# Attention with latent keys on one core: the second part of each exchange issued by ScalarE instead of SyncE

## The reference

```python
q = (x @ wq.T).reshape(B, S, N_HEADS, QK_HEAD)            # QK_HEAD = 128 + 64
q_lat = jnp.einsum('bshd,hdc->bshc', q_nope, wkv_b_h[:, :NOPE])
kv_cache = rmsnorm(kv_lat, kv_norm_w)
scores = (q_lat . kv_cache + q_pe . k_pe) * SCALE          # both einsums over t
attn = jax.nn.softmax(jnp.where(causal, scores, NEG_INF), axis=-1)
out_lat = jnp.einsum('bsht,btc->bshc', attn, kv_cache)
out = jnp.einsum('bshc,hdc->bshd', out_lat, wkv_b_h[:, NOPE:])
return x + out.reshape(B, S, N_HEADS * VDIM) @ wo.T + ffn(xn)
```

## Time and profile before

| | |
|---|---|
| median of 3 runs | 2135.69 us (2128.77 to 2140.19) |
| the profiled execution | 2143.6 us, its span 2141.6 us |
| TensorE's granted clock, mean | 0.915 of 2.4 GHz |
| busy share of the span | PE 84%, DVE 57%, POOL 47%, ACT 40% |
| exchange copies (L943) | 1536, all issued by SyncE: 256 of 64 KB, 768 of 128 KB, 512 of 96 KB |
| DMA queue of SyncE, share of 16 engines | 53.4% |

### The profile page before, as it was taken

How to read it: one execution, slowest core, us unless ns; L and a number is a source line. 1 busy time by engine, 2 the same in 40 slices (tenths; PEclk the granted TensorE clock), 3 DMA queues, 4 the chain that set the end, 5 groups by cost and what they waited for, 6 DMA issues and landing times.

```text
span 2141.6 us, 25543 instructions
## 1 busy us (share of the span) xinstructions
PE 1793.0 (84%) x8174; PEld 1455.8 (68%) x8174; DVE 1214.6 (57%) x2769; ACT 851.5 (40%) x1326; POOL 1003.5 (47%) x634
## 2 busy tenths in 40 slices
PE   6997888787889889778878787888899889898985
PEld 5785677576777667656656576676677667776764
DVE  5764567565666666445455454556555655564652
ACT  4553444333544443333433333333444343434332
POOL 4763445324554554344434444434444454545445
PEclk9888999998999999898989898899999999999988
DMA  6992555646556564553544445455465445644544
GB/s 226 355 312 95 152 151 164 192 112 167 157 134 155 155 181 124 148 136 96 133 117 112 130 112 135 147 133 153 121 152 136 126 116 133 162 111 118 141 115 108
DMA packets 127171, 317.33 MB, mean 148 GB/s; under 512 B 29442, under 2 KB 41987, under 8 KB 125508
## 3 DMA queue, kind: packets, MB, share of 16 engines
q1 hardware_dynamic: 126224, 314.62, 53.4%
q10 hardware_dynamic: 820, 1.15, 0.2%
HBM read 113.28 MB, written 34.60 MB: 69 GB/s over the span
## 4 chain that ended last, share of the span: by engine, by line
issue 24%; PE 23%; SPq 16%; POOL 15%; DVE 7%; ACT 3%; DMA 3%; POOLq 0%; DVEq 0%; ACTq 0%
SPq L943 16%; POOL pT L1312 10%; PE p_out L1075 10%; PE p_score L1057 9%; DVE turned L1145 3%; DMA pT<-turned 2%; POOL qp_l L1301 2%; POOL qp_l L1298 2%; PE p_lat L1037 2%; PE p_result L1087 1%; ACT qp_h L1258 1%; PE p_rot L1037 1%; DVE probs L1122 1%; ACT probs L1225 1%; DVE q_l L1168 1%
## 5 line engine op out<-in xcount | busy, mean ns | idle before, releaser
L1312 POOL TENSOR_TENSOR pT<-pT,pT_h 128x1024 fp32r<-128x1024 f32 x320 | 683.7, 2162 | 484.6 <-ACT pT_h L1237 480.6
L1122 DVE TENSOR_SCALAR_CACHE_REDUCE probs<-p_score 128x512 f32<-128x512 f32 (+3 forms) x640 | 382.0, 602 | 488.2 <-PE p_score L1057 338.6
L1225 ACT ACTIVATE probs<-probs,neg_max 128x128 f32<-128x128 f32 (+15 forms) x256 | 306.9, 1199 | 513.6 <-DVE neg_max L1128 513.3
L1145 DVE STREAM_TRANSPOSE turned<-probs 128x1024 f32<-128x1024 f32 (+7 forms) x384 | 341.8, 915 | 219.6 <-DMA pT<-turned 196.7
L1237 ACT ACTIVATE pT_h<-pT 128x1024 fp32r<-128x1024 f32 x320 | 299.4, 966 | 260.0 <-PE p_out L1075 172.6
L1057 PE MATMUL p_score<-Kn_h,q_h 128*128 128x512 f32 (+3 forms) x640 | 253.9, 397 | 110.5 <-DVE q_l L1168 67.1
L1075 PE MATMUL p_out<-pT_h,V_h 128*128 128x512 f32 (+3 forms) x640 | 256.8, 401 | 57.0 <-POOL pT L1312 56.9
L1087 PE MATMUL p_result<-Wv,o_h 128*128 128x512 f32 x512 | 171.4, 417 | 122.4 <-DVE acc L1187 111.9
L1057 PE MATMUL p_score<-Kp,qp_h 128*128 128x512 f32 (+3 forms) x640 | 244.8, 382 | 10.5 <-POOL qp_l L1301 9.9
L1075 PE MATMUL p_out<-pT_h,V_l 128*128 128x512 f32 (+3 forms) x640 | 248.2, 388 | 0.0
L1075 PE MATMUL p_out<-pT,V_h 128*128 128x512 f32 (+3 forms) x640 | 247.7, 387 | 0.0
(11 more groups left out here) (135 smaller groups left out, 2614.5 us busy)
## 6 DMA issues: line engine op xcount, KB each, us to landing
pT<-turned SPq DMA_DIRECT2D x768, 128.0 KB, 2.3
pT<-turned SPq DMA_DIRECT2D x512, 96.0 KB, 2.1
Wq<-wq_scr SPq DMA_DIRECT2D x63, 512.0 KB, 3.5
Wv<-wv_scr SPq DMA_DIRECT2D x63, 512.0 KB, 4.2
pT<-turned SPq DMA_DIRECT2D x256, 64.0 KB, 2.0
Wp<-wp_scr SPq DMA_DIRECT2D x31, 512.0 KB, 4.4
xT_scr<-xT SPq DMA_DIRECT2D x3, 2048.0 KB, 10.1
xT<-xT_scr SPq DMA_DIRECT2D x3, 2048.0 KB, 10.9
```

Of the source, the lines that this page charges most:

```text
L1122: dve.tensor_scalar(probs[row % ROW_RING][:, b * CW:b * CW + width], p_score[n % SCORE_RING][:, 0:width], SCALE, LOWEST, ALU.mult, ALU.max ...
L1145: last = dve.transpose(to.rearrange("p a t q -> p t a q"), rows.rearrange("p (t a q) -> p t a q", a=4, q=32))
L1225: act.activation(probs[row % ROW_RING][:, 0:width], probs[row % ROW_RING][:, 0:width], ACT.Exp, bias=neg_max[p][:, i:i + 1], scale=1.0, ac ...
L1312: pool.tensor_tensor(low, low.bitcast(F32), high.bitcast(F32), ALU.subtract).then_inc(p_low, 1)
```

## The change

The first part of every exchange stays with SyncE. In chunks three and four the second part is issued by ScalarE, in the same step, in the unit `rotary_add_unit(g)` (7 in chunk three, 8 in chunk four), ahead of anything else of that unit but the query and rotary copies. Waits, semaphores and the 16 DMAs are the same.

```diff
             def step(g):
                 j, h = chunk_of(g), g % H
                 if 1 <= g <= HEADS:
-                    for part in range(parts_of(g - 1)):
-                        exchange(g - 1, part)
+                    exchange(g - 1, 0)
                 if g + 2 < HEADS:
                     load_q(g + 2)
...
+            def exchange_rest(g):
+
+                first, end = part_tiles(g, 1)
+                tiles = slice(tile_base(g) + first, tile_base(g) + end)
+                act.wait_ge(blocked, QB * (g + 1))
+                act.wait_ge(pv_done, free_by(g, end))
+                for a in range(4):
+                    for r in range(4):
+                        act.dma_start(pT[32 * a:32 * (a + 1), r, tiles, :, :].bitcast(F32),
+                                      turned[32 * r:32 * (r + 1), a, tiles, :, :]).then_inc(exchanged[1][g % 2], 16)
...
                     if u == rotary_high_unit(g) and g + 1 < HEADS:
                         high_rotary(g + 1)
+                    if 1 <= g <= HEADS and parts_of(g - 1) > 1 and u == rotary_add_unit(g):
+                        exchange_rest(g - 1)
```

## The result

The changed kernel takes 2182.92 us (median of 4 runs, 2178.62 to 2191.54) beside 2136.64 us for the kernel before: a ratio of 1.0232, 95% interval 1.0204 to 1.0259. It is 46 us slower, where I had forecast 11 us faster, and lies outside the stated range. The profiled execution took 2180.15 us, its span is 2178.3 us, 36.7 us more than that of before.

A forecast was written before the change was run, and what follows sets the result against it. Bound: VectorE's wait for the second part's last copy. Chunk three −27, chunk four +12, tail +4 gave −11 us from 2135.7, so 2125 us; its own range 2113 to 2137, overall range 2095 to 2172.

The forecast's parts named there:

- The rhythm: Landing of the second part's last copy, awaited by VectorE, sets every step's pace; what moves it moves everything.
- When ScalarE gets there: First copy 0.1 us after row 1's exponential starts: 3.9 and 1.0 us earlier in chunk three, nothing on average in four.
- rival (a): ScalarE's first copy waits for the exponential's end, 1.4 or 1.9 us later per step: +51, 2176 us; chance 0.17.
- How fast: ScalarE issues exchange copies at SyncE's 0.63 us each; bounds 2.2 us earlier to 1.6 us later a head.
- Both at once: Chunk three, both queues overlapping for 3.9 and 1.0 us: surplus DMA demand gives back 0.7 us for two heads.
- Rival (b): Descriptor generator serves one queue at a time, so overlapping issues gain nothing: +29, 2165 us; chance 0.18.
- SyncE's loads: Wq and Wp, issued earlier among the last copies, cost 0.4 us a head in chunk three, 0.8 in chunk four.
- What is queued behind ScalarE: Rotary, exponential, query copy and high parts wait behind ScalarE's 10.1 us of issues; covered by about 2 us.
- The tail: Step 64: 16 copies ahead of ScalarE's group 0 make GpSimd start later, ending the kernel 4 us later.
- Rival (c): More is won: surplus only waits (−6), Wq hidden (−18), TensorE idles less; together −43, 2093 us; chance 0.2.

The follow-up runs named there:

- e3: Kernel before, whole exchange on SyncE, but ScalarE issues the Wq and Wp loads in chunks three and four just before copying the next query: 2193.72 us, ratio 1.0268.
- e1: Changed kernel, but SyncE waits for the landing of the second part before issuing Wq and Wp: 2100.04 us, ratio 0.9836 to the kernel before.
- e7: Changed kernel with SyncE's wait before Wq in chunk three only; chunk four as in the kernel before: 2093.35 us, ratio 0.9798.
- e6: Changed kernel, but ScalarE issues only 8 of the second part's 16 copies, SyncE the other 8, then the loads: 2030.92 us, ratio 0.9521.
- e4: Kernel before, plus 16 small 2 KB copies on their own tile issued by ScalarE where the change issues the second part: 2145.99 us, ratio 1.0044.
- e2: Changed kernel, but in chunks three and four ScalarE issues Wq and Wp too, behind its copies on the same queue: 2113.24 us, ratio 0.9899.

## Why the prediction was wrong

**The rhythm: right.** VectorE's wait for the last copy stayed the bound, and what moved that moment moved the time nearly one for one: by 60 us for 61 us of lag in e3, by 72 for 84 between e1 and the changed kernel.

**When ScalarE gets there: right.** Its sequencer did run ahead, by 0.4 us more than I took (1092.05 against the exponential's 1092.37 + 0.1), so rival (a) is out; that its 2176 us lies near the measured time is chance. In chunk three the starts gained what I had counted, in chunk four nothing: 8 x 4.9 = 39 us, and e7, which keeps only that, measured 40. (One of the two starts was misread: 1089.54 + 20.94 − 10.1 is 1100.4 and not 1100.0, so the second kind of step had 1.4 us to win and not 1.0.)

**How fast: right.** 0.64 us a copy (13 in 8.37 us), bounds not needed.

**Both at once: half right.** I had given back 0.7 us for two heads; e7's 40 us leave little room for that, so the surplus mostly waited. Rival (b), one queue at a time, would have left no gain in e7. What the Trainium skill says of one shared generator (Perfetto Trace Analysis, "DMA Instruction — HWDGE (DVE, Sync)") hardly shows at this spacing: in e6 SyncE's 262 copies that were issued while ScalarE issued one took 0.61 us at the median and 0.73 on average, beside 0.59 and 0.61 for the others. The Trainium skill's other sentence, that all queues run on the same 16 DMA engines and interleave (DMA: Bandwidth & Descriptors, "Issuing engines are not separate DMA queues"), is what decided the case, as the windows after show with 0.98 of the engines' time; I had applied it to the copies and not with the same weight to the loads.

**SyncE's loads: this step failed.** "In chunk three a third of the engines' time is free, I take 0.4 us a head; in chunk four [...] I take 0.8 us a head, between nothing and 1.6." The mechanism was named, the term was too small. I let each queue have fair turns, so that the copies would lose little. The lags say that the last copies wait about as long as all the loaded bytes take: +1.7 us with Wq, +3.6 with Wq and Wp, +2.2 at the median in chunk four. Over the 31 steps they add up to 86 us (141.8 − 55.4) in place of 6 + 12 = 18. Taking the loads away measures the same term: the changed kernel loses 46 us and e1 wins 35, so they cost 81 us. What is left of my sum without them, −27 − 6 + 4 = −29, is near e1's −35. The upper bound of 1.6 us covered one load, not two, and I did not believe in it even for one. The windows after have the price: 323 GB/s at a share of 0.98 are 330 GB/s at full, so by my estimate 512 KB fill the engines for 1.6 us and two loads for 3.2. The packets show why that is the cost: no fair turns, but 109 rows of Wq and 90 of Wp in series, with no row of a copy between them.

**What is queued behind ScalarE: nearly right.** e4 puts the whole cost at 11 us, 4.4 of them in the tail, which I had priced at 4, and 4.0 in chunk three, where I had counted the steady state as covered, with 2 us to spare. Which wait lets those 4 us through I did not find.

**The tail: right in kind.** From SyncE's last first part to the end of the span the changed kernel takes 49.3 us (2178.3 − 2129.02), that of before 42.8 (2141.6 − 2098.81): +6.5, against 4. ScalarE's 16 issues took 12.4 us there, and GpSimd began all eight groups behind them.

Rival (c) had its first two gains in e1, once the loads were held back. None of the four rivals said that the loads would cost more than the move could bring.

## What to carry to other kernels

An engine freed from issuing does not become idle: it goes on to whatever stands next in its queue. Ask what that is, how many bytes it moves, and what is in flight on the path at that moment; here a load that nobody waits for cost about its full transfer time when it was issued less than 5 us before the end of the issuing of copies that somebody waits for. One queue had kept the order copies-then-loads for free; with two queues the order has to be written, as a wait (e1) or by keeping the loads behind the last copies on one queue (e2, e6), and then the second queue's issuing time is a real gain.

## What the runs showed that I had not expected

- Where two loads went out on the other queue just before the last copies, VectorE started 5.1 to 5.8 us after the last issue, with one load 3.2 to 3.6 us, beside 1.7 alone: not a fair share but nearly the whole load. The packets of a load went out in one series of 109 of 128, in e3 of 114 of 128 and from the other queue. Rows of 1 KB and of 4 KB gave the same time, and four smaller DMAs, issued over 4 us, gave back about a third of the loss (29 of 81 us). The rule by which the engines choose between two queues stays open beyond that.
- ScalarE's sequencer issued its first copy 0.18 us after the start of an activation that takes 0.60 us (1092.05 against 1091.87), and ahead of the next one: in this kernel DMA issues cost ScalarE's sequencer, not its arithmetic, until the next activation is due.
- The cost of one issue, 0.61 us with a gap of 0.03, was the same for 96 KB as for 2 KB copies (13 in 8.37 and in 8.36 us).
